# Fourth layer's attention: three score buffers of two banks, one bank each for turned tiles and products, copies 1:2 on ACT and DVE, scores of 48 rows in two row groups

## What is computed

```python
q = (x @ Wq + bq).reshape(1, B * N, H, hd)          # H = 16 heads of hd = 16, B * N = 1024
kv = (cond @ Wkv + bkv).reshape(1, -1, 2, H, hd)
k, v = (kv[:, :, 0], kv[:, :, 1])
q = _fq_sym(jnp.transpose(q * scale, (0, 2, 1, 3)), axis=-1)
k = _fq_sym(jnp.transpose(k, (0, 2, 1, 3)), axis=-1)
v = _fq_sym(jnp.transpose(v, (0, 2, 1, 3)), axis=2)
attn = jnp.einsum('bhqd,bhkd->bhqk', q, k)
attn = jax.nn.softmax(attn.astype(jnp.float32), axis=-1)
attn = _fq_unsigned(attn, axis=-1)                  # to 0..255 steps of its row's maximum
out = jnp.einsum('bhqk,bhkd->bhqd', attn, v)
return jnp.transpose(out, (0, 2, 1, 3)).reshape(B, N, C) @ Wp + bp
```

## Time and profile before

| | us |
|---|---|
| three runs | 1419.08, 1412.67, 1414.01 |
| median | 1414.01 |
| span of the profiled execution | 1406.4 |
| the attention's stage in it, first S to last N | 262.8 |
| busy over the span: PE, DVE, ACT, POOL | 989.1, 699.5, 615.9, 126.0 |

### The profile page before, as it was taken

The page is one execution under the profiler, slowest core; times in us unless marked ns, Lnnn a source line. Parts: engine busy times, 40 slices in busy tenths (PEclk is TensorE's granted clock), DMA queues, the critical chain, the costliest instruction groups (busy, mean ns, idle before and its releaser), DMA issues. The chain is left out here.

```text
span 1406.4 us, 18253 instructions
## 1 busy us (share of the span) xinstructions
PE 989.1 (70%) x6772; PEld 614.4 (44%) x6772; DVE 699.5 (50%) x1243; ACT 615.9 (44%) x852; POOL 126.0 (9%) x247
## 2 busy tenths in 40 slices
PE   5269997997934820477726862774777768999998
PEld 3024435664832720133312642443454445666665
DVE  4258745443457750011278682785788763111113
ACT  3026572122347340355546323895899842222221
POOL 0000000000000200000023210110111100300004
PEclk9559997997967965689858985896999977999999
DMA  3211301002000112211100002544311011211102
GB/s 106 90 53 62 102 11 35 0 1 89 1 23 0 61 30 84 89 80 80 40 30 1 1 0 77 147 102 123 101 48 48 1 29 70 82 38 49 40 23 90
DMA packets 45102, 75.17 MB, mean 53 GB/s; under 512 B 4806, under 2 KB 31312, under 8 KB 43264
## 3 DMA queue, kind: packets, MB, share of 16 engines
q1 hardware_dynamic: 40168, 66.79, 15.3%
q0 software_dynamic: 1536, 4.20, 0.9%
q10 hardware_dynamic: 3312, 3.02, 0.6%
HBM read 60.42 MB, written 16.58 MB: 55 GB/s over the span
## 5 line engine op out<-in xcount | busy, mean ns | idle before, releaser
L2108 DVE TENSOR_REDUCE sb_l_NM<-PS 128x1 f32<-128x1024 f32 x128 | 156.1, 1220 | 77.3 <-PE PS L2059 75.7
L2096 ACT ACTIVATE sb_l_E<-PS,sb_l_NB,sb_L3SQS 128x1024 int16<-128x1024 f32 x128 | 154.0, 1203 | 47.5 <-POOL sb_l_NB L2046 47.4
L2059 PE MATMUL PS<-sb_l_K,sb_l_Q 96*128 96x512 bf16 x256 | 85.3, 419 | 59.9 <-ACT sb_l_E L2096 42.0
L713 DVE TENSOR_REDUCE sb_negmax<-PS 128x2 f32<-128x512 f32 x128 | 84.0, 687 | 56.0 <-PE PS L609 54.5
L815 PE MATMUL PS<-sb_Q,sb_K 96*128 96x256 bf16 x256 | 47.0, 316 | 85.7 <-DMA sb_K<-tail 58.7
L2068 PE MATMUL PS<-sb_identb,sb_l_E 128*128 128x128 bf16 x1024 | 87.1, 234 | 22.4 <-ACT sb_l_ET L2101 22.1
L2068 PEld LDWEIGHTS PS<-sb_identb,sb_l_E 128*128 128x128 bf16 x1024 | 71.7, 105 | 71.1 <-issue 57.6
L840 ACT ACTIVATE sb_E<-PS 128x1024 f32<-128x1024 f32 x64 | 65.4, 1023 | 76.2 <-PE PS L815 73.8
L1250 ACT ACTIVATE sb_hidden<-PS 128x512 f32<-128x512 f32 x39 | 23.3, 597 | 165.6 <-PE PS L1204 165.6
L702 ACT ACTIVATE sb_E<-PS 128x1024 f32<-128x1024 f32 x64 | 65.2, 1020 | 59.9 <-PE PS L659 59.5
L1285 DVE TENSOR_TENSOR sb_hidden<-sb_hidden,PS 128x512 f32<-128x512 f32 x39 | 26.8, 687 | 126.2 <-ACT sb_hidden L1250 126.2
(11 more groups left out here) (342 smaller groups left out, 1903.7 us busy)
## 6 DMA issues: line engine op xcount, KB each, us to landing
sb_Q<-q SPq DMA_DIRECT2D x16, 576.0 KB
sb_L3w<-L3w SPq DMA_DIRECT2D x8, 1024.0 KB, 6.6
sb_K<-k SPq DMA_DIRECT2D x24, 192.0 KB
sb_W2E<-L3w SPq DMA_DIRECT2D x8, 512.0 KB, 5.7
k<-sb_tb SPq DMA_DIRECT2D x12, 256.0 KB
sb_l_Q<-q SPq DMA_DIRECT2D x16, 192.0 KB
xs<-zero_row SPq DMA_DIRECT2D x1, 2944.0 KB, 49.1
sb_block_x<-xs SPq DMA_DIRECT2D x23, 128.0 KB, 2.2
```

The source lines that it names most:

```text
L713: dve.tensor_reduce(NM[:, g, 2 * b:2 * b + 2, j:j + 1], core.bank(6 + m % 2).rearrange("p (u k) -> p u k", k=SEQ), axis=AX.X, op=ALU.max, ...
L2059: ins = pe.matmul(core.bank(2 * (n % 2) + half), Q[:, h % RING, t * P:(t + 1) * P], K[:, h % RING, half * HALF:(half + 1) * HALF], start=T ...
L2096: act.activation(E[:, n % 3, :], S(n), ACT.Exp, bias=NB[:, n:n + 1], scale=scale_of(h, t), accum_out=ZS[:, n:n + 1]).then_inc(exped, 1)
L2108: dve.tensor_reduce(NM[:, n:n + 1], S(n), axis=AX.X, op=ALU.max, negate=True).then_inc(maxed, 1)
```

## The change

Six things change in `attention_l3`:

1. Three score buffers of two banks, 0 to 5. S(n) waits for X(n - 3).
2. One bank, 6, for the turned tiles. T(u) waits for the copy of u - 1.
3. One bank, 7, for the products. The first M of a head waits for N of the head before, and N comes one turn earlier on DVE (five turns after the head's last tile).
4. Every third tile (u mod 3 = 1) is copied by ACT, the others by DVE.
5. The scores' contraction has 48 rows. The first 512 keys are multiplied from partitions 0 to 47, the second 512 from partitions 64 to 111. A head has its queries in both places and half of its keys in each, so four loads of half the size take the place of two. Rows are ordered by feature, then part.
6. K isn't cleared any more, and SP doesn't wait for that.

```diff
-    ROWS = 96
+    ROWS, LOWER = 48, 64
...
-    RING = 4
-    ERING, LAG = 3, 4
+    RING, SRING, ERING, LAG = 4, 3, 3, 4
...
-    by_act = [u % 8 in (1, 3, 5, 7) for u in range(NU)]
+    by_act = [u % 3 == 1 for u in range(NU)]
...
-        Q = core.sb(ctx, "l3_Q", [ROWS, RING, TOK], BF16)
-        K = core.sb(ctx, "l3_K", [ROWS, RING, TOK], BF16)
+        Q = core.sb(ctx, "l3_Q", [P, RING, TOK], BF16)
+        K = core.sb(ctx, "l3_K", [P, RING, HALF], BF16)
...
-        S = lambda u: core.PS[:, 2 * (u % 2):2 * (u % 2) + 2, :].rearrange("p b n -> p (b n)")
+        S = lambda u: core.PS[:, 2 * (u % SRING):2 * (u % SRING) + 2, :].rearrange("p b n -> p (b n)")
...
-                sp.wait_ge(cleared, 1)
...
-                    sp.dma_start(Q[:, h % RING, :], qs[h].unsqueeze(0).to_broadcast([ROWS // HD, HD, TOK])
-                                 ).then_inc(q_in[h % RING], 16)
-                    sp.dma_start(K[0:PARTS * HD, h % RING, :], ks[h]).then_inc(q_in[h % RING], 16)
+                    for half in range(2):
+                        rows = slice(LOWER * half, LOWER * half + ROWS)
+                        sp.dma_start(Q[rows, h % RING, :], qs[h].unsqueeze(1).to_broadcast([HD, PARTS, TOK])
+                                     ).then_inc(q_in[h % RING], 16)
+                        sp.dma_start(K[rows, h % RING, :], ks[h].rearrange("(i d) t -> d i t", i=PARTS)
+                                     [:, :, half * HALF:(half + 1) * HALF]).then_inc(q_in[h % RING], 16)
...
-                pool.memset(K[:, :, :].bitcast(F32), 0.0).then_inc(cleared, 1)
...
-                            pe.wait_ge(q_in[h % RING], 32 * (h // RING + 1))
-                        if n >= 2:
-                            pe.wait_ge(exped, n - 1)
+                            pe.wait_ge(q_in[h % RING], 64 * (h // RING + 1))
+                        if n >= SRING:
+                            pe.wait_ge(exped, n - SRING + 1)
                         for half in range(2):
-                            ins = pe.matmul(core.bank(2 * (n % 2) + half), Q[:, h % RING, t * P:(t + 1) * P],
-                                            K[:, h % RING, half * HALF:(half + 1) * HALF], start=True, stop=True)
+                            rows = slice(LOWER * half, LOWER * half + ROWS)
+                            ins = pe.matmul(core.bank(2 * (n % SRING) + half), Q[rows, h % RING, t * P:(t + 1) * P],
+                                            K[rows, h % RING, :], start=True, stop=True)
...
-                        if u >= 2:
-                            wait_turned_out(pe, u - 2)
+                        if u >= 1:
+                            wait_turned_out(pe, u - 1)
                         for k in range(KB):
-                            ins = pe.transpose(core.bank_bf16(4 + u % 2)[:, k * P:(k + 1) * P],
+                            ins = pe.transpose(core.bank_bf16(6)[:, k * P:(k + 1) * P],
...
-                        if t == 0 and h >= 2:
-                            pe.wait_ge(normed, h - 1)
+                        if t == 0 and h >= 1:
+                            pe.wait_ge(normed, h)
                         for k in range(KB):
-                            ins = pe.matmul(core.PS[:, 6 + h % 2, t * HD:(t + 1) * HD], ET[:, u % ERING, k, :],
+                            ins = pe.matmul(core.PS[:, 7, t * HD:(t + 1) * HD], ET[:, u % ERING, k, :],
...
-                for n in range(NU + LAG + 2):
+                for n in range(NU + LAG + 1):
...
-                    u = n - LAG - 2
+                    u = n - LAG - 1
```

More of the change, by code:

```diff
@@ L1997, in attention_l3 @@
     HEADS, HD = 16, 16
-    ROWS = 96
+    ROWS, LOWER = 48, 64
     LN255 = float(np.log(255.0))
     KB = TOK // P
-    RING = 4
-    ERING, LAG = 3, 4
+    RING, SRING, ERING, LAG = 4, 3, 3, 4
     units = [(h, t) for h in range(HEADS) for t in range(NT)]
     NU = len(units)
-    by_act = [u % 8 in (1, 3, 5, 7) for u in range(NU)]
+    by_act = [u % 3 == 1 for u in range(NU)]
     copied_before = lambda u, act: sum(1 for v in range(u) if by_act[v] == act)
     q_in = [core.sem(f"q_in{i}") for i in range(RING)]
-    prefetched, cleared, scored, maxed, biased, exped, turned, out_a, out_v, mixed, inverted, normed = (core.sem(n) for n in (
-        "prefetched", "cleared", "scored", "maxed", "biased", "exped", "turned", "out_a", "out_v", "mixed", "inverted", "normed"))
+    prefetched, scored, maxed, biased, exped, turned, out_a, out_v, mixed, inverted, normed = (core.sem(n) for n in (
+        "prefetched", "scored", "maxed", "biased", "exped", "turned", "out_a", "out_v", "mixed", "inverted", "normed"))
     with ExitStack() as ctx:
-        Q = core.sb(ctx, "l3_Q", [ROWS, RING, TOK], BF16)
-        K = core.sb(ctx, "l3_K", [ROWS, RING, TOK], BF16)
+        Q = core.sb(ctx, "l3_Q", [P, RING, TOK], BF16)
+        K = core.sb(ctx, "l3_K", [P, RING, HALF], BF16)
         E = core.sb(ctx, "l3_E", [P, 3, TOK], I16)
@@ L2085, in copy_out @@
                     eng.wait_ge(mixed, u - ERING + 1)
-                return ET[:, u % ERING].rearrange("p k q -> p (k q)"), core.PS[:, 4 + u % 2, :].bitcast(I16)
+                return ET[:, u % ERING].rearrange("p k q -> p (k q)"), core.PS[:, 6, :].bitcast(I16)
             @block.scalar
@@ L2119, in _ @@
                         dve.tensor_tensor(core.XN[:, :, h * HD:(h + 1) * HD],
-                                          core.PS[:, 6 + h % 2, 0:NT * HD].rearrange("p (t d) -> p t d", d=HD),
+                                          core.PS[:, 7, 0:NT * HD].rearrange("p (t d) -> p t d", d=HD),
                                           RZ[:, h * NT:(h + 1) * NT].unsqueeze(2).to_broadcast([P, NT, HD]),
```

## The result

The changed kernel takes 1497.97 us (median of 4 runs, 1494.61 to 1502.15) against 1414.68 us for the kernel before (4 runs). The ratio is 1.0576, with a 95% interval of 1.0529 to 1.0623: slower by 5.8%, 83 us. I had predicted 1494 us. The profiled execution after has a span of 1493.5 us and took 1495.24; the median lies 4.5 us above that span, where before it was 7.6.

A forecast was written before the change was run, and what follows sets the result against it. A loop of waits through scores, maximum, copies and exponential, with no engine full, bounds the fourth attention at 1.86 us a tile. Terms 62.6 + 13 + 0 - 1 - 8 + 13 = +80 on 1414.0 give 1494 us, range 1460 to 1522.

The forecast's parts named there:

- The loop of the single bank: Fourth attention: waits for the one turned bank close a loop over three tiles, 7.04 us a round; +62.6 us.
- side conditions: Within that loop: DVE's copy ends before the second maximum must start, and T(3) is done before the next copy.
- Head's end: With one product bank, a head's first product waits for the previous head's N; +13 us, ends 0 and 22.
- Row groups: Score matmul pair in two row groups: 0 us, between -9 if run together and +9 if one after the other.
- Clock: Attention stage's granted TensorE clock falls from 0.89 to 0.8: +13 us, ends -3 and +37.
- The stop: PE's 13.8 us mid-group stop, read as instructions behind the xs clearing, shrinks to 5.5 us: -8, ends -13.8 and 0.
- Loads: Before the first scores: no clearing of K, but four loads instead of two; -1 us, ends -1.8 and +1.
- my 7.43: Pace of the attention loop in the kernel before: 7.43 us for four tiles, 1.86 each.
- Rival A: Same single-bank loop, PE at half clock nearly throughout: +100 us, 1514, with slow row groups 1523; chance 0.10.
- C: Rival: smaller loop, DVE's copy not in the way, 1.99 us a tile; 1434 us with heads' ends; chance 0.04.
- D: Rival: turned-bank wait ends before PE comes to it, DVE sets 1.60 us a tile; -33 us, 1381; chance 0.04.
- E: Rival: no change, new waits and gain cancel, 1414 us; chance 0.02.

The follow-up runs named there:

- e1: Kernel before with one bank for the turned tiles instead of two, nothing else changed: 1554.85 us, ratio 1.085.
- e7: Changed kernel with all copies on DVE, the single turned bank staying: 1426.53 us, ratio 1.0068 to the kernel before.
- e4: Changed kernel with the banks of before (two score buffers, two turned, two product banks): 1423.59 us, ratio 0.9973 to the kernel before.
- e5: Kernel before with one product bank, and N one turn earlier on DVE: 1437.54 us, ratio 1.0194.
- e2: Kernel before with scores in two row groups of 48 rows, four loads a head, K not cleared: 1419.23 us, ratio 0.9898.
- e12: Kernel before with scores of 48 rows in one group, one after the other: 1443.75 us, ratio 1.0229.
- e3: Changed kernel with scores of 96 rows in one group, K cleared, two loads a head: 1524.29 us, ratio 1.0655 to the kernel before.
- e8: Kernel before with the transfer that clears xs issued behind the thirteenth head's load instead of the seventh's: 1420.44 us, ratio 1.0034.
- e10: Kernel before with row groups and the clearing of xs cut into 16 transfers: 1391.11 us, ratio 0.9853.
- e11: Kernel before with only the clearing of xs cut into 16 transfers, no row groups: 1396.24 us, ratio 0.9901.
- e9: Kernel before with row groups and the clearing of xs issued behind the thirteenth head's load: 1415.35 us, ratio 1.0.
- e6: Kernel before with copies shared 1:2 between ACT and DVE instead of 1:1: 1415.02 us, ratio 1.0024.

## Why the prediction was right, point by point

**The loop of the single bank** (+62.6). Right in kind: e1 shows it alone, e7 takes ACT out of it and nearly all of the loss with it, e4 takes the bank out. In size the loop was 7.65 us a round instead of 7.04. The difference of 0.61, 26 us over 42.7 rounds, is the half clock, which also led the loop through T and its copy on DVE. There one of the prediction's side conditions failed: T(3), which it had at about 1.5 us after T(2), came at 1.89, and its S at 3.03, too late for the second maximum to follow the copy on DVE.

**Head's end** (+13). The three heads of 64.0 us are 24 tiles of 2.55 and 2.8 us more, so 14 to 15 us over the stage. The pattern is the forecast one too: the five ends with a wait of 0.70 cost nothing, and the ten with 1.31 carry it. As a part alone (e5) it cost 22 to 27 us, with a lower clock in it.

**Row groups** (0, between -9 and +9). The two matmuls run at once, and M to S takes 0.34 us against 0.26, so a wait for the array to empty adds at most 0.08 us between products and scores. Between scores and turns none shows: in e2 T starts 0.55 us after S, before the modelled end of the pair. Of the two rules of the Trainium skill that I set against each other (TensorEngine Tiling (Array Packing), Key Properties), the trace agrees with that of independent tiles (the pair in 0.61 us, where one after the other takes 1.03 in e12). The drain shows as no more than those 0.08 us; e12 has the same 0.34, so they may as well come from the 48 rows. The 0 was a middle between two rules, and the 0.1 to 0.2 us that it gave the wait for the array stood in no row of before; it came out near enough: at half clock the pair is 0.4 us shorter, which the forecast had not counted.

**Clock** (+13, at a granted clock of 0.8). Mis-sized: the clock was 0.50, so the loop took the whole 26 us. Outside its pace and its stop, the stage before has 262.7 - 239.2 - 13.8 = 9.7 us (ends, half-clock stretches), the stage after 352.3 - 341.4 - 8.5 = 2.4, so by difference 7 of the 26 come back: +19 net. I had put the low clock down to longer waits alone. e2 and e12 show that the 48-row scores bring it down by themselves. That +19 lies near +13 is luck: the clock was forecast far too high, and a round at half clock was priced at 0.83 us where it cost 0.61, because the same edit made S 0.4 us shorter at that clock. With 96 rows (e3) the stage was 364.0 us, at a clock of 0.63.

**The stop** (-8). It shortened by 5.3 us. The place was right: PE came to it 34.8 us after the issue, forecast 34. That the stop hangs on the transfer to xs is shown by e8, e10 and e11. That its end is a fixed time after the issue is not so: it was 39.6 us before, 43.3 after, and 27.3 and 49.8 for the two stops of e8. All of these stops begin while the transfer runs, which takes 49 us from issue to landing (the line's size and median time in the kernel before):

```profile
xs<-zero_row SPq DMA_DIRECT2D x1, 2944.0 KB, 49.1
```

That what PE waits for is its instructions is argued, not shown.

**Loads** (-1). From the first load's issue, at 869.91, to the first S, at 874.08, it now takes 4.2 us. What the loads won is read from PE's idle time before the first S: 15.1 us instead of 17.8, so -2.7, outside the stated ends of -1.8 and +1. In the other kernels it is 14.9 to 15.3 with four loads and no clearing (e2, e4, e7, e9, e10) and 17.4 to 17.9 with two loads and the clearing of 96 rows (e1, e3, e5, e6, e8, e11). The clearing is 1.8 of it; the rest was not taken apart.

**Sum.** Loop 26 + 62.6, head's ends 15, the pace of before slightly over my 7.43 (-1.4), ends and old clock losses -7.3, stop -5.3: +89.6 in the stage, and 2.5 less in the span: +87.1. In the medians it is +83 to +84, because the median after lies 4.5 us over its profiled span and not 7.6. Forecast +80. Rival A (half clock throughout, 1514) was right in its condition, but its price left out that S would be shorter. C, D and E are out by the pace of the heads.

## What to carry to other kernels

A buffer's count says little before one has asked who empties it and what stands ahead of him in his queue. Here the kernel with one bank for the turned tiles (and one for the products) took 0.2 us a tile more than before when DVE did all the copies, and 0.8 more when every third copy stood behind the exponential. A loop written out from pitches of the old trace, in queue order, gave the new pace to within 8%; most of the rest was the clock, so a forecast for a PE stage needs both levels worked out. And rows of zeros in a contraction may be paying for something: taking them away left TensorE at 1.2 GHz, and one group of 48 rows was 2.3% slower than 96 (e12).

## What the runs showed of the hardware that I had not expected

- The granted clock of the stage was 0.50 to 0.57 in all seven kernels with 48-row scores (0.50 in the changed kernel, e2, e7 and e12); with 96-row scores it was 0.56 (e1) and 0.63 (e3) in the slow loops and 0.78 to 0.93 in the others (0.93 in e11). The 48-row scores did not rule out full clock altogether: in stretches of 20 us it reached 0.64 in e4, 0.76 in e9 and 0.67 in e10. In e12 PE was busy 92% of the stage and stayed at 1.2 GHz.
- Two score matmuls on rows 0 to 47 and 64 to 111 took 0.61 us together at half clock; two of 48 rows in one group, one after the other, took 1.03.
- In all twelve kernels that clear xs by one transfer of 2.9 MB in rows of 1 KB, PE stopped for 5 to 15 us without a releaser in the 50 us behind its issue, and in six of them (e1, e2, e4, e8, e9, e12) a second time, for 3 to 12 us. In 16 pieces, spread over the heads, the same data stopped PE for no more than 2 us and gave 1%.
